# Two changes to a fused two-layer kernel: the batch loop of the second attention written out, and the weights of the last feed-forward cut by groups of inner steps

## The reference, cut to what matters

```
x = x + tanh(g_xattn[0]) * L0_xattn(layernorm(x), ctx, mask)   # 16 batches x 256 rows, 16 heads of 128
x = x + tanh(g_ffn[0])   * L0_ffn(layernorm(x))                # mixture of 8 experts, 2 for each row
x = x + tanh(g_xattn[1]) * L1_xattn(layernorm(x), ctx)         # second attention, 16 heads of 32
x = x + tanh(g_ffn[1])   * L1_ffn(layernorm(x))                # last feed-forward

def L1_xattn(x, y):   # the last 16 rows of ctx have weights of their own
    q = ln(x @ Wq + bq); k, v = ln(y_main @ Wk + bk), y_main @ Wv + bv
    k_dca, v_dca = ln(...), ...                                 # of the 16 rows
    return (softmax(q k.T / sqrt(32)) v + softmax(q k_dca.T / sqrt(32)) v_dca) @ Wo + bo

def L1_ffn(x):        # x: 4096 rows of 512, hidden 2048
    h = gelu(x @ proj1.T + proj1_bias)
    return h @ proj2.T + proj2_bias
```

## Time and profile before

| | us |
|---|---|
| runs before | 3873.36, 3881.41, 3882.3 (median 3881.41) |
| the profiled execution itself | 3879.29 |
| its span, from first to last instruction | 3877.4 |
| PE busy in the span | 3617.4 (93%) |
| DVE busy | 2296.4 (59%) |
| ACT busy | 1838.5 (47%) |
| POOL busy | 1536.2 (40%) |
| second attention, loop of batches | from about 2370 to about 2937 |
| last feed-forward | from about 3097 to the end |

### The profile page before, as it was taken

One profiled execution on the slowest core, in us unless ns is written; L12 is line 12 of the kernel. 1 busy time (PEld: TensorE's weight loads), 2 busy tenths in 40 slices (PEclk: granted clock), 3 DMA queues, 4 the chain that ended last, 5 costly groups with the idle time before them and its releaser, 6 DMA issues. The chain is left out here.

```text
span 3877.4 us, 70183 instructions
## 1 busy us (share of the span) xinstructions
PE 3617.4 (93%) x23276; PEld 3121.9 (81%) x23276; DVE 2296.4 (59%) x5703; ACT 1838.5 (47%) x4718; POOL 1536.2 (40%) x1517
## 2 busy tenths in 40 slices
PE   7999999999999995999999938999889779999999
PEld 7999999999999995999999826666666457777777
DVE  6666666566666664767676668888888342222221
ACT  4445545544444442555555417777777432222222
POOL 3333333534444443656565536666665320000000
PEclk9999999999999997999999969999999789999999
DMA  4466565336665624566666631111111020000000
GB/s 155 175 229 220 203 230 215 109 122 224 218 224 213 215 93 180 218 236 239 233 242 228 223 136 46 54 50 50 52 51 32 25 104 22 22 22 22 22 22 22
DMA packets 225043, 523.31 MB, mean 135 GB/s; under 512 B 12402, under 2 KB 25203, under 8 KB 220291
## 3 DMA queue, kind: packets, MB, share of 16 engines
q1 hardware_dynamic: 118402, 297.01, 21.8%
q10 hardware_dynamic: 96224, 190.92, 13.3%
q0 software_dynamic: 10272, 33.63, 2.6%
HBM read 270.39 MB, written 251.13 MB: 135 GB/s over the span
## 5 line engine op out<-in xcount | busy, mean ns | idle before, releaser
L671 POOL TENSOR_SCALAR a_prob<-a_prob,a_rinv 128x256 f32<-128x256 f32 x512 | 471.4, 931 | 836.1 <-DVE a_rinv L854 836.1
L618 ACT ACTIVATE a_prob<-a_prob,a_low_bias 128x256 f32<-128x256 f32 x512 | 256.5, 502 | 458.8 <-DVE a_low_bias L845 458.8
L1173 DVE TENSOR_TENSOR e_w_lo<-e_w_raw,e_w_hi 128x1024 fp32r<-128x1024 f32 (+1 forms) x316 | 381.4, 1248 | 42.5 <-ACT e_w_hi L1131 41.9
L2139 DVE TENSOR_TENSOR f_h_lo<-f_h_f,f_h_hi 128x512 fp32r<-128x512 f32 x128 | 92.1, 720 | 458.8 <-ACT f_h_hi L2115 458.8
L1079 PE MATMUL e_gb<-e_xt_hi,e_w_hi 128*128 128x256 f32 x1248 | 355.6, 285 | 5.7 <-DVE e_xt_lo L1173 5.7
L1080 PE MATMUL e_gb<-e_xt_lo,e_w_hi 128*128 128x256 f32 x1248 | 355.3, 285 | 0.0
L1081 PE MATMUL e_gb<-e_xt_hi,e_w_lo 128*128 128x256 f32 x1248 | 355.3, 285 | 0.0
L1063 POOL TENSOR_TENSOR e_act_hi<-e_act_f,e_zeros 128x256 fp32r<-128x256 f32 x156 | 233.9, 1500 | 281.8 <-DVE e_act_f L1193 281.8
L2113 ACT ACTIVATE f_h_f<-f_hb,f_b_sb 128x512 f32<-128x512 f32 x128 | 88.1, 688 | 486.2 <-PE f_hb L2038 426.4
L421 PE MATMUL a_pj<-a_xt,a_wq_hi 128*128 128x256 f32 x1024 | 310.0, 303 | 0.9 <-DVE a_q_lo L704 0.9
L423 PE MATMUL a_pj<-a_xt,a_wq_lo 128*128 128x256 f32 x1024 | 289.2, 282 | 0.0
(11 more groups left out here) (343 smaller groups left out, 11290.2 us busy)
## 6 DMA issues: line engine op xcount, KB each, us to landing
e_w_raw<-in_w_gate SPq DMA_DIRECT2D x41, 2048.0 KB, 7.6
x_sorted<-a_blank ACTq DMA_DIRECT2D x42, 1792.0 KB, 6.5
y_sorted<-a_blank ACTq DMA_DIRECT2D x42, 1792.0 KB, 8.7
e_w_raw<-in_w_out SPq DMA_DIRECT2D x41, 1024.0 KB, 5.6
e_xg<-x_sorted SPq DMA_DIRECT2D x41, 512.0 KB, 8.2
y_sorted<-e_y_sb SPq DMA_DIRECT2D x39, 512.0 KB, 2.8
xt_rows<-a_xt SPq DMA_DIRECT2D x16, 1024.0 KB, 5.2
a_xt<-xt_rows SPq DMA_DIRECT2D x16, 1024.0 KB, 5.3
```

The source lines that it names most:

```text
L618: e = nc.scalar.activation(prob[:, u % 4, t], prob[:, u % 4, t], ACT.Exp, bias=low_bias[:, u % 2, t:t + 1], scale=-1.0, accum_out=rsum[:, ...
L671: p = nc.gpsimd.tensor_scalar(prob[:, u % 4, t], prob[:, u % 4, t], rinv[:, u % 2, t:t + 1], None, ALU.mult)
L1173: return nc.vector.tensor_tensor(out, raw, hi.bitcast(F32), ALU.subtract)
```

## The change

It has two parts that do not depend on each other.

1. In `all_steps` of the second attention the loop over pairs of batches becomes a loop of Python, so the 6 x 16 steps stand one behind the other in each engine's stream. SP's own loop, which issues the loads of this stage, stays a loop. Every semaphore value becomes a constant.
2. In the feed-forward the pieces of `w1` are cut by groups of four inner steps (512 of its 2048 columns, all input rows) and alternate with those of `w2`; the first `hidden` needs piece 0 alone. The rows of x are loaded first. The inverse root is one POOL operation (`pow` with -0.5) on a variance that DVE writes, in every chunk. DVE makes the low parts of pieces 0 and 1, POOL those of the six others, now during the first chunk, and PE waits for a piece where its group of steps starts. The gate and the bias of the residual come later in ACT's and DVE's streams.

```diff
-            with eng.Fori(0, B // 2 - 2) as i:
+            for i in range(B // 2 - 2):
                 for u in range(AHEAD, AHEAD + LOOP):
                     step(i, u)
...
-        pieces = [(w1[:, c:c + 1], w1_hi[:, c:c + 1], w1_lo[:, c:c + 1]) for c in range(FC)]
-        pieces += [(w2[:, h:h + W2_STEPS], w2_hi[:, h:h + W2_STEPS], w2_lo[:, h:h + W2_STEPS]) for h in range(0, HC, W2_STEPS)]
-        ROOM = (0, 1, 2, 1, 2, 1, 1, 1)
+        STEPS = 4
+        pieces = []
+        for h in range(0, HC, STEPS):
+            cols = slice(h * P, (h + STEPS) * P)
+            pieces += [(w1[:, :, cols], w1_hi[:, :, cols], w1_lo[:, :, cols]), (w2[:, h:h + STEPS], w2_hi[:, h:h + STEPS], w2_lo[:, h:h + STEPS])]
+        SPLIT = {0: 2, 1: 3, 3: 4, 6: 5, 8: 6, 10: 7}
+            rows = w_raw[:] if n not in (1, 2) else (x_sb[:, 1] if n == 1 else xn[:]).rearrange("p t d -> p (t d)")
...
-        NORM = {2: 0, 3: 1, 4: 2, 5: 3, 6: 4}
+        NORM = {2: 0, 3: 1, 5: 2, 6: 3}
...
+            load_rows(0, 0)
+            load(0)
+            sp.dma_start(ident[:], identity).then_inc(id_loaded, 16)
+            load(1)
             for dst, src in consts:
                 sp.dma_start(dst, src).then_inc(c_loaded, 16)
+            low_done(sp, 0)
+            load(3)
+            low_done(sp, 1)
+            load_rows(1, 1)
+            sp.wait_ge(t_ready, FC)
+            load(2)
+            for n in range(4, len(pieces)):
+                low_done(sp, n - 1)
+                load(n)
...
             def first():                                  # PE
                 for c in range(FC):
                     turn(0, c)
-                for n in range(FC):
-                    low_done(pe, n)
+                low_done(pe, 0)
                 hidden(0, 0, 0)
...
+                        if is_first and (j + 1) % STEPS == 0:
+                            low_done(pe, 2 * ((j + 1) // STEPS))
                         hidden(n, b, j + 1)
...
-                    if is_first and j % W2_STEPS == 0:
-                        low_done(pe, FC + j // W2_STEPS)
+                    if is_first and j % STEPS == 0:
+                        low_done(pe, 2 * (j // STEPS) + 1)
                     out(n, j)
...
             def first():                                  # ACT
-                for n in range(FC):
-                    split(n)
+                split(0)
+                act.wait_ge(c_loaded, 16 * len(consts))
+                nc.scalar.activation(gate_t[:], gate_t[:], ACT.Tanh).then_inc(gate_done, 1)
+                split(1)
                 for c in range(FC):
                     turned(0, 0, c)
-                split(FC)
...
-                    if is_first and j % W2_STEPS == 1 and j + W2_STEPS < HC:
-                        split(FC + 1 + j // W2_STEPS)
+                    if is_first and j in SPLIT:
+                        split(SPLIT[j])
...
+            def root(n):                                  # POOL
+                pool.wait_ge(link_done, LINKS * n + 3)
+                pool.nop(nofuse=True)
+                nc.gpsimd.tensor_tensor(rstd[:], var[:], power[:], ALU.pow).then_inc(root_done, 1)
+            def chunk(i, b, last, is_first=False):
+                if is_first:
+                    split(2)
+                    split(3)
+                if not last:
+                    root(2 * i + b + 1)
+                if is_first:
+                    for n in range(4, len(pieces)):
+                        split(n)
...
             def first():                                  # DVE
-                for n in range(2):
-                    dve.wait_ge(w_hid, n + 1)
-                    low(pieces[n][2], raw(n), pieces[n][1]).then_inc(w_lod, 1)
-                dve.wait_ge(w_lod, 1)
-                for part in NORM.values():
-                    normalize(0, 0, part)
+                normalize(0, 0, 0)
+                normalize(0, 0, 1)
+                split(0)
+                normalize(0, 0, 2)
+                split(1)
                 for c in range(FC):
                     turned(0, 0, c)
+                dve.wait_ge(gate_done, 1)
+                V.tensor_scalar(b2_sb[:], b2_sb[:], gate_t[:, 0:1], None, ALU.mult).then_inc(bias_done, 1)
+                dve.wait_ge(bias_done, 1)
+                normalize(0, 0, 3)
```

More of the change, by code:

```diff
@@ L1952, in feed_forward @@
         stats, mv, rstd = sb("stats", [P, TC, 6]), sb("mv", [P, TC, 2]), sb("rstd", [P, TC])
-        root = [sb(f"root{n}", [P, TC]) for n in range(3)]
+        var, power = sb("var", [P, TC]), sb("power", [P, TC])
         xt_hi, xt_lo = sb("xt_hi", [P, 2, FC, CH], F32R), sb("xt_lo", [P, 2, FC, CH], F32R)
@@ L1970, in feed_forward @@
         o_ready, o_done = sem("o_ready"), sem("o_done")
-        consts = [(ident[:], identity), (b1_sb[:], b1), (b2_sb[:], b2), (gate_t[:], gate)]
-        W2_STEPS = 4
-        pieces = [(w1[:, c:c + 1], w1_hi[:, c:c + 1], w1_lo[:, c:c + 1]) for c in range(FC)]
-        pieces += [(w2[:, h:h + W2_STEPS], w2_hi[:, h:h + W2_STEPS], w2_lo[:, h:h + W2_STEPS]) for h in range(0, HC, W2_STEPS)]
-        ROOM = (0, 1, 2, 1, 2, 1, 1, 1)
+        consts = [(b1_sb[:], b1), (gate_t[:], gate), (b2_sb[:], b2)]
+        STEPS = 4
[4 more added lines that the diff above has]
+        SPLIT = {0: 2, 1: 3, 3: 4, 6: 5, 8: 6, 10: 7}
         def raw(n):
-            a = pieces[n][0].shape[1]
-            rows = (xn[:].rearrange("p t d -> p (t d)"), w_raw[:], x_sb[:, 1].rearrange("p t d -> p (t d)"))[ROOM[n]]
-            return rows.rearrange("p (a b) -> p a b", a=a)
+            rows = w_raw[:] if n not in (1, 2) else (x_sb[:, 1] if n == 1 else xn[:]).rearrange("p t d -> p (t d)")
+            return rows.rearrange("p (a b) -> p a b", a=STEPS)
         def low_done(eng, n):
@@ L1991, in low_done @@
                 eng.wait_ge(w_lod_pool, n - 1)
-        NORM = {2: 0, 3: 1, 4: 2, 5: 3, 6: 4}
+        NORM = {2: 0, 3: 1, 5: 2, 6: 3}
         TURN = {7 + c: c for c in range(FC)}
+        LINKS = 4
         def all_chunks(eng, first, chunk):
@@ L2062, in out @@
                         mm.then_inc(o_ready, 1)
-            pe.wait_ge(c_loaded, 16 * len(consts))
+            pe.wait_ge(id_loaded, 16)
             def first():
@@ L2128, in _, with split @@
         def _(pool):
-            for n in range(2, len(pieces)):
+            nc.gpsimd.memset(power[:], -0.5).then_inc(power_set, 1)
+            pool.wait_ge(power_set, 1)
+            def root(n):
+                pool.wait_ge(link_done, LINKS * n + 3)
+                pool.nop(nofuse=True)
+                nc.gpsimd.tensor_tensor(rstd[:], var[:], power[:], ALU.pow).then_inc(root_done, 1)
+            def split(n):
                 pool.wait_ge(w_hid, n + 1)
                 nc.gpsimd.tensor_tensor(pieces[n][2], raw(n), pieces[n][1].bitcast(F32), ALU.subtract).then_inc(w_lod_pool, 1)
+            def chunk(i, b, last, is_first=False):
[7 more added lines that the diff above has]
+                        split(n)
+            all_chunks(pool, lambda: root(0), chunk)
         @block.vector
@@ L2135, in _ @@
             V = nc.vector
-            LINKS = 2 + ROOT_LINKS + 1
             def low(out, raw_in, hi):
@@ L2165, in normalize @@
                     l.then_inc(link_done, 1)
-                    inverse_root(dve, V, link_done, at + 2, mv[:, :, 1], LN_EPS, root, rstd[:], 0)
+                    dve.wait_ge(link_done, at + 2)
+                    V.tensor_scalar(var[:], mv[:, :, 1], LN_EPS, None, ALU.add).then_inc(link_done, 1)
                 elif part == 2:
-                    inverse_root(dve, V, link_done, at + 2, mv[:, :, 1], LN_EPS, root, rstd[:], 1)
-                elif part == 3:
+                    dve.wait_ge(root_done, n + 1)
+                    if isinstance(n, int) and n == 1:
+                        low_done(dve, 2)
                     for t in range(TC):
```

25 lines of the change are left out of this document (8 added, 17 removed).

## The result

| us | before | after |
|---|---|---|
| runs of the first comparison | 3873.36 to 3882.56, median 3881.86 | 3809.48, 3810.49, 3811.25, 3820.68, median 3810.87 |
| profiled execution, its span | 3879.29, 3877.4 | 3811.25, 3809.5 |

The ratio is 0.9827 (0.9806 to 0.9849): 71 us faster by the medians, 68.0 by the two profiled executions. One of the four executions after took 10 us more than the others; no trace of it was taken.

A forecast was written before the change was run, and what follows sets the result against it. PE, busy 93% of the span, was taken as the bound, so gains come from its idle or low-clock stretches: 3879.3 - 32.0 (attention loop) - 13.5 (feed-forward start) = 3833.8 us, range 3818 to 3866.

The forecast's parts named there:

- the short batch as the floor: Attention loop: batches alternate 50.01 and 44.41 us; eleven at 44.41 would be 488.5, leaving 36.2 us excess.
- One long wait left: Attention written out: one of six 6.0 us waits stays, 30.2 us gained; bounds none left (36.2), three left (18.1).
- the counted block starts: Attention, DVE: 8 KB code blocks, read as 128 instructions, start in steps 7, 2, 4, 6, never between reciprocal and L1805.
- Register instructions, 0.15 us a batch: Attention: removing compare-and-branch and register instructions gains 0.15 us for each of 12 batches, 1.8 us; bounds 0 and 0.66.
- The loop's branch acquitted, the code's place accused: Attention loop: branch takes at most 0.21 us, no code fetched; place in code shifts DVE by tens of nanoseconds.
- a distance of 0.12 against 0.20 us: Attention: L1385 starting 0.12 us after POOL's L1724 takes 4.31 us, at 0.20 it takes 0.17.
- The start of the feed-forward, 13.5: Feed-forward's start: first hidden matmul comes 13.5 us sooner, 21.6 instead of 35.1 after SP's first DMA; bounds 9 and 17.
- The power in later chunks, 0: Feed-forward's later chunks: POOL's power instead of DVE's linked operations lies under PE's work, 0 us.
- Late pieces, 0: Feed-forward's first chunk: later weight pieces are ready in time, cost 0; with cover gone for every piece, 13.5 us.
- The collision that stays: Rival, attention: the loop goes but the long waits of every second batch stay, 3864 us; chance 0.17.
- all batches long: Rival, attention: every batch becomes a long one, +36 us there, 3900 us in all; chance 0.07.
- the starved first chunk: Rival, feed-forward: attention gains, but late pieces in the first chunk give the feed-forward's gain back, 3847 us; chance 0.12.

The follow-up runs named there:

- dve_late10: Kernel after with ten one-column memsets on VectorE ahead of L1387: 3839.4 us, ratio 0.9905 against before.
- pow_loop: Kernel after with the second attention's inverse root as a power on GpSimd, but that attention's loop kept: 3805.5 us, ratio 0.9813 against before.
- pow_att: Kernel after with the second attention's inverse root made as a power on GpSimd instead of linked VectorE operations: 3804.7 us, ratio 0.9811 against before.
- loop_pad: Kernel before, loop kept, with eight empty instructions on VectorE inside the loop's body: 3850.6 us, ratio 0.9927 against before.
- loop_pre8: Kernel before, loop kept, with eight empty instructions on VectorE ahead of the loop: 3879.3 us, one run.
- loop_rot4: Kernel before, loop kept but cut four steps later, body holding steps 12 to 27 instead of 8 to 23: 3837.6 us, ratio 0.9899 against before.
- pool_busy8: Kernel after with eight one-column memsets on GpSimd ahead of L1724 in the step where the root begins: 3811.1 us.
- ffn_pow: Kernel before with only the feed-forward's root changed, to one power on GpSimd instead of VectorE's linked operations: 3875.7 us, one execution.
- ffn_only: Kernel after with the attention loop of before, so only the feed-forward is changed: 3861.7 us, ratio 0.9957 against before.

## Why the prediction was wrong, step by step

- **The failing step: the short batch as the floor.** The sum took 44.41 us as what a batch costs and allowed 0.15 (at most 0.66) below it. It is 43.13: 1.2 us of the short batch were L1387's lost race, which `dve_late10` puts back, and about 0.1 the loop. Twelve times 1.28 are 15.4, of which the sum held 1.8: 13.6 of the 20.8 us that the attention brought beyond its term. The upper bound came from one batch behind the loop, 43.75, in which L1387 takes 0.59 us by the trace of before and pays half of the price: the one batch of 43.7 us in after has it at 0.60. The row was in the trace and I did not compare L1387 across the three kinds of batch, as I had compared L1385.
- **One long wait left.** None is left in the trace after, 6.0 us. The remaining 1.2 are a net of small pieces; the largest, 2.6 us at the stage's end, is the luck of this trace (68.4 against 71.1 us from the last batch's first scores on, where every other kernel with the loop written out took 70.8 to 72.4). L1902 stood 0.21 us behind the reciprocal in the fifth step of every batch, as said. That the counted block starts are the reason is not shown: the count took 8 KB from one instruction queue, while the other one moved 26 packets with 0.43 MB after, 16 KB each, and which queue is VectorE's stands in no row.
- **Register instructions, 0.15 us a batch.** `pow_loop` against `pow_att`: 0.13. Right. The cost of fetches, 0: ten of the eleven batches lie within 0.05 us of each other beside 48 packets of code, so at most the 0.6 us of the one longer batch.
- **The loop's branch acquitted, the code's place accused.** Right, by `loop_pad`, `loop_pre8` and `loop_rot4`. That the shift of some 60 ns passes through L1805 to L1385 is right too. The last link, a distance of 0.12 against 0.20 us, is not the rule (`pool_busy8`).
- **The start of the feed-forward, 13.5.** 14.1. Counted from SP's first DMA: x 5.8 us for 5.7, the statistics' end 8.2 (8.2), normalized rows begin 12.7 (13.0) and take 1.91, first hidden matmul 21.0 (21.6).
- **The power in later chunks, 0.** It gave 3.9 us, by `ffn_pow`; the forecast put it at nothing, under PE's work, without a row for that. **Late pieces, 0.** They cost 2.0 us in the trace of after: from the first gelu to the seventeenth its first chunk took 94.2 us, with the old pieces and the power (`ffn_pow`) 92.2. But in eleven of the thirteen traces with the new pieces it took 92.8 to 93.0, so the usual price is 0.6 to 0.8. In after VectorE's low parts of h stand beside GpSimd's split, two of them take 4.78 us instead of 1.4, and PE waits behind them; in `ffn_only`, the same feed-forward, the split comes 1.4 us earlier from the first gelu, beside one low part, and PE does not wait there.

```profile
3092.52 4.66 POOL L2149 TENSOR_TENSOR f_w_lo<-f_w_raw,f_w_hi 128x2048 fp32r<-128x2048 f32 x1 [3.42 <-ACT f_w_hi L2104]
3093.72 4.78 DVE L2168 TENSOR_TENSOR f_h_lo<-f_h_f,f_h_hi 128x512 fp32r<-128x512 f32 x2 [5.77 <-ACT f_h_hi L2125]
3097.88 0.47 PE L2047 MATMUL f_ob<-f_w_hi,f_h_hi 128*128 128x512 f32 x1 [1.48 <-DVE f_h_lo L2168]
```

- **The rivals.** The collision that stays (3864) and all batches long (3900) did not come; the starved first chunk came as a 2.0 us piece of itself. No rival stood below the forecast: I had a mechanism for more loss and none for more gain, although the race's logic gives both.

## What to carry to other kernels

Before a "good" iteration serves as the floor, compare every small operation in it with its own shortest time anywhere in the trace; one that takes 1.07 us here and 0.15 there is a race that the good iteration loses too. A gain that comes from engines missing each other by tens of nanoseconds belongs to the race and not to the edit: removing the racing operations gave as much as writing the loop out, with the loop kept, and left 0.13 us a batch as the loop's price. And a pause of empty instructions is no test of such a race until the trace shows that the engine moved.

## What the hardware showed unexpectedly

- Eight empty instructions inside a loop's body moved the kernel by 29 us (3850.6 against 3879.4), and 8 or 64 ahead of it by nothing. They moved a late start of VectorE (0.06 to 0.09 us in each later turn, 0.3 in the first) from behind the reciprocal to ahead of it.
- Empty instructions hardly hold an engine up: three on VectorE moved L1387 by nothing, two on GpSimd moved L1724 by 0.065 us. One-column memsets moved it 0.008 us each on VectorE up to six.
- L1385 took 0.30 us at 0.05 us behind L1724 with memsets ahead of it, and 4.31 at 0.12 with the gather straight ahead.
- The power on GpSimd on 128x2 took 0.72 us in the attention, 1.01 on 128x4 in the feed-forward and 0.94 on 128x2 in the first attention.
